# Feed-forward chunks as two products of 256 columns in the two halves of a PSUM bank, in place of one of 512

## The reference

```
x = x + 0.5 * ffn(layernorm(x))      # 8 experts, top 2, each 256 x 256
x = x + attn(layernorm(x))           # 16 heads of 16, rotary, softmax
x = x + 0.5 * ffn(layernorm(x))

ffn:  logits = x @ Wr.T;  top-2 of 8, softmax over the two
      a token beyond an expert's capacity (1537 per sequence) is dropped there
      out = sum over the two chosen experts of w * (x @ We[e])
```

## Time and profile before

| | |
|---|---|
| time, median of three | 6255.09 us |
| span of the profiled execution | 6262.1 us |
| first-stream products L373 | from 28.7 to 577.1 us |
| last-stream products L1668 | from 5796.4 to the end |
| PE busy | 6192.5 us (99%) |
| PEld busy | 2761.4 us (44%) |
| DVE busy | 5912.5 us (94%) |

### The profile page before, as it was taken

The page is one execution under the profiler, slowest core; times in us unless marked ns, Lnnn a source line. Parts: engine busy times, 40 slices in busy tenths (PEclk is TensorE's granted clock), DMA queues, the critical chain, the costliest instruction groups (busy, mean ns, idle before and its releaser), DMA issues. The chain is left out here.

```text
span 6262.1 us, 158145 instructions
## 1 busy us (share of the span) xinstructions
PE 6192.5 (99%) x54276; PEld 2761.4 (44%) x54276; DVE 5912.5 (94%) x6787; ACT 4861.3 (78%) x8953; POOL 399.2 (6%) x604
## 2 busy tenths in 40 slices
PE   8998999999999999999999999999999999999999
PEld 6886333333333333333333333333333333333787
DVE  7998999999999999999999999999999999992777
ACT  4443488888888888888888888888888888887221
POOL 3443100000000000000000000000000000000222
PEclk9999799999999999999999999999999999998999
DMA  2335010101010101010101010101010101000110
GB/s 84 124 117 141 19 17 14 17 14 17 14 17 14 17 14 17 14 17 14 17 14 17 14 17 14 17 14 17 14 17 14 17 11 20 3 22 21 59 54 33
DMA packets 121414, 175.92 MB, mean 28 GB/s; under 512 B 62016, under 2 KB 78944, under 8 KB 117728
## 3 DMA queue, kind: packets, MB, share of 16 engines
q1 hardware_dynamic: 120928, 168.25, 11.8%
HBM read 98.47 MB, written 69.73 MB: 27 GB/s over the span
## 5 line engine op out<-in xcount | busy, mean ns | idle before, releaser
L1197 DVE TENSOR_REDUCE at_mx<-at_m 128x1 f32<-128x1024 f32 x4027 | 4928.1, 1224 | 44.4 <-PE at_m L1031 24.5
L1163 ACT ACTIVATE at_ex<-at_s 128x512 f32<-128x512 f32 x8192 | 4447.6, 595 | 630.8 <-PE at_s L1052 103.3
L1052 PE MATMUL at_s<-at_q,at_k 50*128 50x512 f32 x8192 | 2994.5, 446 | 3.4 <-ACT at_ex L1163 3.2
L1031 PE MATMUL at_m<-at_k,at_q 48*128 48x512 f32 x8032 | 2926.0, 443 | 0.0
L1062 PE MATMUL at_po<-at_ex,at_v 128*32 128x256 f32 x32816 | 2632.1, 393 | 1.6 <-ACT at_o L1153 1.6
L1031 PEld LDWEIGHTS at_m<-at_k,at_q 48*128 48x128 f32 x8032 | 1183.8, 185 | 1656.8 <-DVE at_mx L1197 1593.5
L1062 PEld LDWEIGHTS at_po<-at_ex,at_v 128*32 128x32 f32 x32816 | 647.6, 108 | 1486.0 <-issue 753.0
L1052 PEld LDWEIGHTS at_s<-at_q,at_k 50*128 50x128 f32 x8192 | 1210.6, 185 | 53.1 <-ACT at_ex L1163 36.5
L993 POOL COPY at_v<-at_vst 128x1024 f32<-128x1024 f32 x16 | 16.7, 1043 | 4460.4 <-DMA at_vst<-v_by_head 4460.2
L1668 PE MATMUL bk_ps<-sh_weh,bk_xl 128*128 128x512 f32 x512 | 168.7, 411 | 6.8 <-DVE bk_acc L1717 3.9
L1668 PE MATMUL bk_ps<-sh_wel,bk_xh 128*128 128x512 f32 x512 | 159.7, 393 | 0.0
(11 more groups left out here) (216 smaller groups left out, 2918.4 us busy)
## 6 DMA issues: line engine op xcount, KB each, us to landing
at_q<-q_parts SPq DMA_DIRECT2D x96, 256.0 KB, 5.0
at_k<-k_parts SPq DMA_DIRECT2D x96, 256.0 KB, 6.2
q_parts<-fr_parts SPq DMA_DIRECT2D x64, 256.0 KB, 2.2
k_parts<-fr_parts SPq DMA_DIRECT2D x64, 256.0 KB, 2.5
attended<-at_o SPq DMA_DIRECT2D x256, 34.0 KB
fr_x<-in_x SPq DMA_DIRECT2D x16, 512.0 KB, 4.3
after_ffn<-fr_acc SPq DMA_DIRECT2D x16, 512.0 KB, 3.0
v_by_head<-fr_v SPq DMA_DIRECT2D x16, 512.0 KB, 4.4
```

Of the source, the lines that this page charges most:

```text
L1031: ins = pe.matmul(pm[w][:, h * QB:(h + 1) * QB], Q[p][rows, base + i * P:base + (i + 1) * P], K[p][rows, c * CW + h * QB:c * CW + (h + 1) ...
L1052: pe.matmul(ps[event(t) % NS], K[p][rows, j * P:(j + 1) * P], Q[p][rows, sb_ * QU + g * QB:sb_ * QU + (g + 1) * QB], start=True, stop=True ...
L1163: ac.activation(Ex[QUAD * (j % NX) + slot][:, :], ps[event(t) % NS], ACT.Exp)\
L1197: ve.tensor_reduce(out=mx[u][:, i, c:c + 1], in_=first[(RED + k) % len(first)][:, 0:CW] if opens else pm[w][:, :], op=ALU.max, axis=AX.X)\
```

## The change

In both streams the six products of 512 columns become twelve of 256. The loop over the two experts of the chunk is now outermost: the six products of the first expert go into columns 0 to 255 of the bank, then the six of the second into columns 256 to 511. The same parts of x are loaded, once for each expert. The start flag is set on the first product of each half, the stop flag on its last. The wait before the chunk, the increment of s_mm after it, and the code of the other engines are as they were.

```diff
-                        for t, (a, b) in enumerate(SPLIT):
-                            for c in range(NC):
-                                last = pe.matmul(pe_s[BANK[n]][:, :], (xh, xl)[a][0][u][:, c, i * P:(i + 1) * P],
-                                                 (weh, wel)[b][:, c, EP * k:EP * (k + 1), :].rearrange("p e f -> p (e f)"),
-                                                 start=(t == 0 and c == 0), stop=(t == len(SPLIT) - 1 and c == NC - 1))
+                        for e in range(EP):
+                            for t, (a, b) in enumerate(SPLIT):
+                                for c in range(NC):
+                                    last = pe.matmul(pe_s[BANK[n]][:, e * D:(e + 1) * D], (xh, xl)[a][0][u][:, c, i * P:(i + 1) * P],
+                                                     (weh, wel)[b][:, c, EP * k + e, :],
+                                                     start=(t == 0 and c == 0), stop=(t == len(SPLIT) - 1 and c == NC - 1))
                         last.then_inc(s_mm, 1)
```

More of the change, by code:

```diff
@@ L1665, in experts @@
                             pe.wait_ge(s_ac, g * STEPS + EP * (last_use + 1))
[L1666 to L1670, removed]
+                        for e in range(EP):
+                            for t, (a, b) in enumerate(SPLIT):
+                                for c in range(NC):
+                                    last = pe.matmul(pe_s[BANK[n]][:, e * D:(e + 1) * D], (xh, xl)[a][u][:, c, i * P:(i + 1) * P],
+                                                     (weh, wel)[b][:, c, EP * k + e, :],
+                                                     start=(t == 0 and c == 0), stop=(t == len(SPLIT) - 1 and c == NC - 1))
                         last.then_inc(s_mm, 1)
```

## The result

The kernel with the change takes 6279.09 us (median of six runs, 6274.26 to 6285.25); the kernel before, beside it, 6257.26 (6253.89 to 6264.44). The ratio is 1.0034 with a 95% interval of 1.0023 to 1.0045, which is 14 to 28 us more. The prediction was 6248, with a range up to 6268. It was wrong: the change makes the kernel slower, and by more than the range allowed.

A forecast was written before the change was run, and what follows sets the result against it. PE was taken to bound the feed-forward phases, with DVE close behind in front; attention is bound by DVE. Front 5.0 plus back 2.1 made 7.1 us less, 6255.1 to 6248.0 us; forecast 6243 to 6253, full range 6240 to 6268.

The forecast's parts named there:

- doubling the number of products and loads for the same columns costs nothing by this row: Feed-forward chunks: the values' row, 24 products of 256 columns in 2.72 us, prices the new products at 0.1133 each.
- the 1.36 us for twelve: Forecast time of a changed chunk, twelve products of 256 columns, saving 0.035 to 0.04 against the slower 512-column rate.
- Two rates of streaming, 0.227 and 0.233: Feed-forward products of 512 columns: even back groups stream at 0.227 us each, front and odd back groups at 0.233.
- only the buffer of x differs: Back's even and odd groups, 1.365 against 1.40 us a chunk: no wait explains it, only x's buffer differs.
- The bounds: Range for twelve new products from the values' fastest and slowest rows: 1.36 us, or 1.41 to 1.46; 1.36 was taken.
- Rival 2: Feed-forward chunks: weight loads become the pace, 1.41 a chunk giving 6265 us, 1.46 giving 6284; chance 0.14.
- Rival 1: Feed-forward products: a fixed time per product, at most 0.0083 us; half of it gives 6257 us; chance 0.20.
- Rival 3: Chunks 3 and 7: PE is the only limit, waits give way, all chunks count: 14 us less, 6241; chance 0.06.
- its +7.7 us: Skill's rule against the change: fixed 2.5 ns per product, 6 more products in 512 chunks, 7.7 us more.
- The path in front: Front groups: only chunks 3 to 13 shorten the period, 0.385 us a group; other savings lengthen chunk 3's wait; 5.0 taken.
- issue: PE's queue: 12 products and 12 loads in 1.36 us, 8.8 products a us; attention already takes 9.9, so no limit.
- The waits: PE's waits for DVE: front chunk 3's load idle longer than 0.28 us; back's even chunk 7 loses what PE gained.

The follow-up runs named there:

- m1: Separate kernel, PE alone on ones at the kernel's SBUF addresses, then places moved: front 231.9 and 118.8 ns for 512 and 256 columns, values 113.4.
- e3: The changed kernel plus unused SBUF padding, putting x 64 bytes ahead of the expert weights: 6258.73 us, ratio 1.0000 to the kernel before.
- m2: Separate kernel, PE alone on ones: 64 residue pairs at 512 and 256 columns, three places at six widths; 256 columns took 113.3 to 120.0 ns.
- m3: Separate kernel, PE alone: 256-column products behind seven predecessors, then shorter loads; 113.3 or 117.8 ns at x 32, w 224, always 120.0 at 224, 224.
- e5: The kernel before (512 columns) plus padding only, putting x 64 bytes ahead of the expert weights: 6262.46 us, ratio 1.0004 to the kernel before.
- e4: The kernel before (512 columns) plus 352 bytes of padding, putting x and expert weights at equal residues: 6249.56 us, ratio 0.9989 to the kernel before.
- e1: The change in the front stream alone, back as in the kernel before: 6267.29 us, ratio 1.0019 to the kernel before.
- e6: Kernel before with front in halves, x 64 bytes ahead of weights, and back in 512 columns at equal residues, by padding: 6260.07 us, ratio 0.9997.

## Why the prediction was wrong

**The step that failed** is "doubling the number of products and loads for the same columns costs nothing by this row", and with it the 1.36 us for twelve. The row was a true row of the same operation, but of other places: the values have x 64 bytes ahead of w, where the delay is 0. The experts' operands have 4.3 to 6.7 ns a product (117.6 to 120.0 less 113.3). Shown by m1 (PE alone at the same addresses gives the same paces) and by e3 (the same instructions, moved by padding, run at 113.3 in most of front and in part of back, and the runs are no longer slower).

**"Two rates of streaming, 0.227 and 0.233"** was wrong too. The map is described by one rate and a delay per product: 0 to 8.5 ns on 512 columns, 0 to 6.7 on 256 (m2). The prediction's own remark, "only the buffer of x differs", named the cause, and took it as a property of the wide products that halves would escape. A cause tied to the buffer had to be asked of the new products too. I did not look up the addresses.

**The bounds.** The pace of rows 12, 0.1175, gave 1.41 a chunk as an upper bound, and I set it aside since the row in mid-group was nearer in time. In the kernel after it is 1.41 to 1.44. By m3 it is most likely the second steady pace of such a place (x 64 ahead of w); that was not tried at the values' own addresses. It was the only row of before in which a delay shows at 256 columns.

**The rivals.** Rival 2 was nearest in what it said: a slowdown of 5 ns "(buffers that collide, as the parity in back may be)" that shows in full, twelve times a chunk. Its first price, 6265 for 1.41 a chunk, was 17 us above my 6248; at 1.42 to 1.44 the kernel is at 6279. I gave it 0.14. Whether the load or the stream gives way, no run tells. Rival 1 had the form, a time per product of up to 8 ns, but it is a time of the place, not of the product. Rival 3's gain did not come, since nothing became faster.

**A rule of the Trainium skill.** The paces seen are 113.3 ns and up for 256 columns and 226.7 and up for 512, twice as much, and the extra time on 256 columns is 0 to 6.7 ns by place (m2). The Trainium skill, "TensorE: Matmul & The Clock Gate", section "Back-to-back issue gap", has N / 2.4 + 2.5 ns, which it calls the isolated gap; that is 109.2 and 215.8, below every pace of these products. The sign that it gave came true and its +7.7 us, an estimate, was too small; a fixed term, the same at every place, is not what the runs show.

**What held.** The path in front held in part. From the start of chunk 3 to that of chunk 14 PE needs 0.34 us more in an even group and 0.27 in an odd one. In an even group the period grows by 0.30, about that: the rest still goes into the wait at chunk 3. In an odd group it grows by 0.43: the wait there is used up, PE alone sets the time, and chunks 14, 15, 0, 1 and 2 count too. The prediction had read that wait in an odd group alone and took it for both. That all chunks count once a wait is used up is rival 3's mechanism, reached from the other side. The mean of the two is the 0.37 measured. Back: 16 x 0.08 = 1.28 in an even group, less what the waits at chunks 7, 15 and 0 gave back, 0.84 measured; in an odd one 16 x 0.02 = 0.32, measured 0.34. So the sign of each phase follows from the one term, and in the traces the groups bring some 14 us. Clock in the groups, DVE and the number of products did as they were said to; issue did too, but for the one stop before group 12. The waits went the other way, as they must: shorter, since PE became slower.

## What to carry to other kernels

Before taking the price of a new product from a like one in the trace, compare where both have their operands: here the residues of stationary and moving operand modulo 256 bytes set 113 to 120 ns for the same instruction. An unexplained difference between two equal pieces of code, such as a parity, is a mechanism that the change may multiply, so settle it first. Where PE sets the end, padding is an edit worth trying alone: 352 bytes gave 0.9989 [0.9980, 0.9998], a gain just told from none, and the best place has to be found again for each width and looked up for every operand that the padding moves.

## What the runs showed of the hardware

- A product with its own load of 128 columns, fp32r operands, at the full clock: at best 113.3 ns for 256 columns and 226.7 for 512, in none of the 64 pairs of residues less (m2). A place adds 0 to 6.7 ns to each product of 256 columns and 0 to 8.5 to each of 512, with a period of 256 bytes in either operand (m1). At 192 columns the place adds nothing: 111.7 ns at three places.
- Equal residues are best for 512 columns (226.7 in the kernel) and worst for 256 (120.0); with x 64 bytes ahead it is 233.3 (e5) and 113.3, but 117.8 where w lies at 128 or 160 (m2, e4).
- One place can have two steady paces (113.3 and 117.8 at x 32, w 224), and one product of 512 columns ahead is enough to bring the slower one for 48 products (m3).
- An edit can show far behind its own code: PE stands still for 2.0 to 2.6 us in back, with no wait that the profile names, in all four kernels with halves in front and in none of the four without; two of the four (e1, e6) have back as before. The cause is open.
